# A stack of eight layers on one core: the V products of the biased attention, one half in every step instead of both halves in every second one

## The reference, cut to what matters

```
L0:  causal softmax(q k^T / 4) v                      (rotary q, k; rows see earlier keys only)
L1:  softmax over all keys of (q k^T / 4 + bias[h, j-i]) v (bias from 32 buckets of the distance j-i)
```

## Time and profile before

| what | us |
|---|---|
| runs of the kernel | 7314.04, 7329.81, 7330.81 (median 7329.81) |
| the profiled execution, its own time | 7322.16 |
| its span, first to last instruction | 7320.5 |
| V products of the biased attention, first and last start | 2835.0, 3802.2 |
| TensorE busy, whole span | 5981.8 (82%) |
| VectorE busy, whole span | 4653.9 (64%) |
| ScalarE busy, whole span | 2690.0 (37%) |

### The profile page before, as it was taken

The page is one execution under the profiler, slowest core; times in us unless marked ns, Lnnn a source line. Parts: engine busy times, 40 slices in busy tenths (PEclk is TensorE's granted clock), DMA queues, the critical chain, the costliest instruction groups (busy, mean ns, idle before and its releaser), DMA issues. The chain is left out here.

```text
span 7320.5 us, 109988 instructions
## 1 busy us (share of the span) xinstructions
PE 5981.8 (82%) x31088; PEld 3331.2 (46%) x31088; DVE 4653.9 (64%) x11759; ACT 2690.0 (37%) x6018; POOL 1326.5 (18%) x1059
## 2 busy tenths in 40 slices
PE   5799868989987977888863588987996888998979
PEld 2344344655565542222222353334553456554755
DVE  4666567733863657888867648984335775447735
ACT  0166524712462203666640105541110255224711
POOL 1211115100621021000000005540002441016100
PEclk9799989989998988999996799998998899999989
DMA  4333255662466433232312221124222456324641
GB/s 140 92 78 78 59 153 155 192 197 74 140 190 192 126 116 100 71 83 72 82 52 91 88 77 42 37 59 116 70 67 82 129 163 208 97 88 151 197 151 57
DMA packets 914604, 807.21 MB, mean 110 GB/s; under 512 B 241768, under 2 KB 770113, under 8 KB 913857
## 3 DMA queue, kind: packets, MB, share of 16 engines
q1 hardware_dynamic: 502064, 507.31, 23.7%
q10 hardware_dynamic: 389888, 274.83, 12.1%
q0 software_dynamic: 22144, 18.99, 0.8%
HBM read 506.25 MB, written 316.67 MB: 112 GB/s over the span
## 5 line engine op out<-in xcount | busy, mean ns | idle before, releaser
L1428 ACT ACTIVATE Catt_E<-Catt_t 128x512 f32<-128x512 f32 x1024 | 571.4, 595 | 387.9 <-DVE Catt_t L1391 287.3
L1377 DVE CUSTOM_DVE_ANT_0 Catt_S<-Catt_s,Catt_win 128x1024 f32<-128x1024 f32 x512 | 621.0, 1215 | 12.2 <-DMA Catt_win<-skewed 10.6
L1377 DVE CUSTOM_DVE_ANT_0 Aatt_S<-Aatt_s,Aatt_win 128x128 f32<-128x128 f32 (+7 forms) x512 | 373.2, 756 | 184.9 <-PE Aatt_s L1298 181.1
L1327 PE MATMUL Catt_t<-Catt_Q,Catt_K 123*128 123x512 bf16 x1024 | 354.6, 386 | 145.1 <-ACT Catt_E L1428 111.9
L1428 ACT ACTIVATE Aatt_E<-Aatt_t 128x512 f32<-128x512 f32 (+3 forms) x768 | 335.0, 493 | 215.2 <-PE Aatt_t L1330 135.7
L1391 DVE TENSOR_TENSOR Catt_t<-Catt_t,Catt_near 128x256 f32<-128x256 f32 (+2 forms) x640 | 287.8, 458 | 137.4 <-PE Catt_t L1327 133.3
L1298 PE MATMUL Catt_s<-Catt_K,Catt_Q 96*128 96x512 bf16 x1024 | 320.8, 396 | 28.5 <-DMA Catt_K<-k_parts 14.8
L2399 PE MATMUL scan_cum<-scan_X,scan_upto 128*128 128x512 f32 x512 | 266.6, 611 | 26.0 <-DVE scan_X L2468 24.3
L1327 PEld LDWEIGHTS Catt_t<-Catt_Q,Catt_K 123*128 123x128 bf16 x1024 | 96.7, 97 | 410.3 <-ACT Catt_E L1428 325.5
L2397 PE MATMUL scan_cum<-scan_X,scan_after 128*128 128x512 f32 x448 | 242.2, 623 | 39.9 <-DVE scan_pi L2479 39.9
L1349 PE MATMUL Catt_o<-Catt_E,Catt_V 128*32 128x256 f32 x4096 | 274.1, 385 | 0.0
(11 more groups left out here) (728 smaller groups left out, 14158.8 us busy)
## 6 DMA issues: line engine op xcount, KB each, us to landing
moe_cb<-c_s SPq DMA_DIRECT2D x16, 1024.0 KB
skewed<-lines POOLq DMA_DIRECT2D x8, 1920.0 KB
Catt_win<-skewed SPq DMA_DIRECT2D x16, 960.0 KB, 4.7
rec<-state_in_r ACTq DMA_DIRECT2D x32, 416.0 KB
scan_r<-rec SPq DMA_DIRECT2D x64, 208.0 KB, 2.4
Catt_near<-near_s SPq DMA_DIRECT2D x32, 384.0 KB
Aatt_Rb<-r_s ACTq DMA_DIRECT2D x32, 256.0 KB
v_s<-B0qkv_vo ACTq DMA_DIRECT2D x32, 256.0 KB, 2.1
```

Of the source, the lines that this page charges most:

```text
L1327: ins = t.matmul(bank(it, n)[:, 0:hi - lo], K[:, b, h, kb * P:(kb + 1) * P], Q[:, b, h, lo:hi], start=True, stop=not diagonal)
L1377: v.tensor_tensor_reduce(out=S[:, j % 2, 0:w], in0=s_ps[j % 2][:, 0:w], in1=win[:, 0 if causal else h, w0:w0 + w], scale=-1.0, scalar=BIG, ...
L1428: a.activation(E[:, kb % NB, h, lo:hi], bank(it, n)[:, 0:hi - lo], ACT.Exp, scale=scale).then_inc(exped, 1)
```

## The change

One argument of TensorE's list differs. In the causal stage nothing is changed. In the biased stage `values` is called itself, in every step: step i's half c = i % 2, 8 records, behind `scores` and `scores_by_key` of the same step of the list.

```
-            written_out(t, PAIRS, ST, ((0, scores), (TURN, turn_maxima), (LAG, scores_by_key), (LAG + 3, values_of_block)))
+            written_out(t, PAIRS, ST, ((0, scores), (TURN, turn_maxima), (LAG, scores_by_key), (LAG + 3, values_of_block if causal else values)))
```

## The result

The changed kernel took 7249.56 us in the median of four runs (7245.08 to 7261.63), the kernel before 7321.93 (7306.64 to 7330.81). The ratio is 0.9906, with a 95% interval of 0.9883 to 0.9929: 0.7 to 1.2% faster. In a second series, on one chip with other kernels, it was 7257.73 against 7313.87, ratio 0.9922 (0.9909 to 0.9934). The forecast was 7263 us, reckoned from a median before of 7329.8; a fourth run, of 7306.64, has since moved that median to 7321.93.

The account below looks back on a forecast made before the run. VectorE plus its waits for TensorE's t bounds the biased stage. Gains of 1.22 + 0.86 + 0.13 = 2.21 us over 30.2 batches give 67 us: 7329.8 - 67 = 7263 us, range 7234 to just short of 7320.

Parts of the forecast that it names:

- V stands in front of the odd t: Biased stage: seven of VectorE's eight waits per batch come from 16 V products queued before an odd step's t.
- The price of a half: TensorE, biased stage: each further V batch costs 0.23 us, 1.8 us per batch of 16 steps.
- Rival A: Further V batches are not hidden and TensorE's order carries the chain: 56 us slower, 7386 us; chance 0.13.
- First kind of pair: Step pairs with the addition in the row's second half: waits vanish, pair takes 3.38 us instead of 3.66.
- Second kind of pair: Step pairs with the addition in the row's first half: 0.43 us each off waits of 0.62 and 0.55, 0.26 whole.
- The cover is exactly used up: Second kind of pair: next even step's t and its bank both come at 3414.15, leaving a margin of 0.00.
- new waits at even steps: Sign against the forecast: additions at even steps of the biased stage begin to wait.
- rival B: Gain halved by late t of even steps, with ScalarE's DMA issues left out: 33 us, 7297 us; chance 0.15.
- The step with two additions: Biased stage, wait of 0.26 us at 3390.88: bounds 0 and 0.26, middle of 0.13 us taken as gain.
- Sum: Biased stage, per batch: 1.22 + 0.86 + 0.13 = 2.21 us of 30.4 gone, 67 us over 30.2 batches.

Follow-up runs that it names:

- the half rows: Kernel before, with the c=0 half of each V row left out in the biased stage for all key blocks but the first; ratio 0.9939.

## Why the prediction was right

*The step "V stands in front of the odd t".* Right for six of the seven waits. Moving the row moved them, halving it in either of two ways removed them or most of them. The seventh, 0.62 us in front of the mask of phase 15, does not come from V's length in front of t: the half rows still have 0.61 there, and it is gone with the copy out six steps later.

*The price of a half.* Right to the hundredth: 495 of the 508 half batches take 0.57 us from their first weight load to the next load of another product. Going in costs 0.32 against 0.22 us as before, so the price of a further batch is the 0.23 us of the sum, and the trace agrees with the rule of the Trainium skill on the drain (TensorEngine Tiling (Array Packing), Key Properties) in kind, with that number; that it is a drain that takes the time, no run shows. That nearly all of these 1.8 us per batch is hidden is shown by the half rows, which have none of them and a median batch shorter by only 0.13 us. Rival A is out.

*First kind of pair.* Right: 1.97 + 1.68 us of mask distance became 1.68 + 1.68, as replayed. The waits of 0.27, 0.28 and 0.41 us are gone.

*Second kind of pair.* This is the term that was mis-sized. I counted 0.43 + 0.43 + 0.26 = 1.12 us per batch; the six places of that kind together got 0.58 us shorter. Two things were missing. "The cover is exactly used up" was too kind: at the change from one kind to the next and within it, t c=0 behind the half batch came 0.25 and 0.12 us late, new waits at even steps, which the prediction had named as a sign of its being wrong; both vanish with V between the two t. And of the last odd wait only 0.13 us went, because ScalarE's copy out and DMA issue stand in front of that exponential: it went to nothing only when these were moved away. I had named these issues in rival B as left out.

*The step with two additions.* 0.13 us taken; the four places about it (phases 0 to 3) sum to 0.17 us less. Right in sum, but as -0.41 and +0.38 in neighbouring steps, where ScalarE issues four stores; with the stores moved away the second of the two waits fell from 0.43 to 0.06 us. So this term was luck: I had followed neither chain.

*Sum.* 1.75 us a batch instead of 2.21. Over 30.2 batches that is 53 us, and the stage gave 56.8, for 67 forecast: 0.85 of it. The 4 us between are single long stalls, of which the kernel before had more: a batch in the mean was 30.61 us and is 28.71. (A mask distance before of 1.91 us, as the prediction has it, is that mean; 30.4 over 16 is 1.90.) That the first medians lie 72 us apart, beyond the forecast, I put down to scatter of the untouched stages (18.5 us in the one pair of profiles), and so it is in part luck that the time came so near to the forecast; the second series, 7313.87 to 7257.73, has 56 us, what the stage gave. By the stage, the truth lay between the forecast and rival B (33 us).

## What to carry to other kernels

When an in-order engine works ahead of the bounding one, count how much work stands between two of the pieces that the bounding engine waits for; splitting a long row in two helps there even at a higher total cost, as long as the engine has the room. Two uses of the same code can answer the same edit in opposite ways: the biased stage with two o banks won 57 us, the causal one with one bank lost 50. The banks are not the whole difference, since the biased stage with one bank for o and three for t, as in the causal stage, still won 47; what else there is was not tested. A replay is good to a tenth of a microsecond only if it has every queue in it, DMA issues and the slow helper engine too.

## What the runs showed of the hardware that was not expected

A row of products on quarters of the array lasts as long as its fullest quarter: 8 records in two quarters took 0.99 us, 8 in four quarters 0.57, 16 in four 1.00.

Issuing DMAs holds up ScalarE's own work: the issue of the sums' DMA takes it 0.54 us in front of an exponential, and in the stretches told above three stores in a row took 2.37 us in the half rows and 2.18 in the changed kernel, where one takes 0.45 in the median.

With nearly half of the V records left out, the granted clock from 2900 to 3680 us was 0.98 in the mean instead of 1.00; in the stretch shown TensorE had been busy 1.27 of the 3.0 us before it fell. With three banks for t and its 2.5 us waits the mean was 0.97, with the copy out later and its wait of nearly 4 us in each batch 0.92. These kernels are therefore slower than their chains alone would make them, the last one by more than a little.
